# New order tables for the steady passes of a two-block transformer kernel

## The chip, the cores and the metric

One core of one Trainium2 chip runs the kernel. The time is device microseconds (us) of one execution. Three runs of the kernel before gave a median of 767.87 us (767.48 to 768.92). The trace is of one profiled execution of 767.54 us.

## The reference

Two transformer blocks work on 8 batches of 256 tokens with 256 channels. Each block adds attention and a feed-forward layer, both of the same normalised input, to its residual.

```python
xn = _layernorm(x, axis=-1)
x = x + _L0_attn_ref(xn, ...) + _L0_ffn_ref(xn, ...)
xn = _layernorm(x, axis=-1)
x = x + _L1_attn_ref(xn, ...) + _L1_ffn_ref(xn, ...)
```

- Block 0 attention: 16 heads of 16 channels, scores with an ALiBi bias and a causal mask, softmax clamped at 1e-10, output projection.
- Block 0 feed-forward: 8 experts, `silu(x @ Wg) * (x @ Wu) @ Wd`, summed with router weights that come from a sigmoid, two exponentials and a top-2 choice.
- Block 1 attention: 16 heads, causal, with biases.
- Block 1 feed-forward: two ternarised linear layers (256 to 1024 to 256) with an exact GELU between them. Its output is quantised with the largest magnitude over all batches, so that part comes at the very end.

## The kernel before, in words

The work of one batch is cut into named **steps**, and each engine (PE = TensorE matmuls, DVE = VectorE, ACT = ScalarE, POOL = GpSimd, SP = SyncE, which issues the DMAs) does its own part of each step. A step's parts are tied by semaphores only, so the order in which an engine takes its steps is free as long as nothing waits in a circle. This order is written out by hand: `ORDER_TEXT` has for each of tensor, vector, scalar and gpsimd four lists, `first`, `steady`, `last` and `final`. `run_passes` runs `first` once, `steady` six times in a loop, then `last` and `final`. SP follows the tensor list.

A steady pass is software-pipelined: it holds block 0 of batch n, block 1 of batch n-1, and, marked with `+`, the start of block 0 of batch n+1. Every engine takes its list strictly in order, and the loop goes round from the list's end to its head.

The number behind a step's name in the text does not bind: `in_turn` sorts the steps of one name and writes them back into that name's places. `score:5 norm:1 score:6` at a list's head therefore means score 0, norm 0, score 1. Only the sequence of names counts.

The steps that matter here:

- `ln1a`, `ln1b`: layer norm statistics (DVE), the power for 1/std and the bias sum (POOL), the normalising (DVE, line 1370). `ln1a` needs the last `down` of the pass before. `tr1` turns the result on PE (line 1085); ACT copies it to `xt_hi` (954), DVE takes the remainder `xt_lo` (1375). `q1`, `k1` (1111), `w1` (1160) and `v1` (1124) read both.
- `score`: PE computes two heads at a time (1193, 1195), the pair counted on the even step; DVE adds the bias and takes row maxima (1524), ACT exponentiates (1013). A pair's matmuls wait until DVE has read the pair before. `norm` (DVE, 1546 and 1549), `turn` (PE transposes, 1203 to 1205, and an ACT copy, 1022), `value` (PE, 1253) follow. `b` is block 1's first score round (DVE line 1538), `s` its second (PE 1222 to 1228, ACT 1041, a POOL mask 865), `m` and `mp` carry its row maxima, `y` its values (PE 1253 and 1259, DVE reciprocal 1557).
- `gate`, `up` (PE 1138; ACT tanh 990; DVE 1470 and 1475; ACT 994; POOL 856) and `down` (PE 1149; DVE 1486): one expert each, 0 to 7. `rt1` (DVE 1403 to 1410) and `rt2` (two ACT exponentials, 985 and 986, then 21 small DVE instructions, 1425 to 1464): the router.
- `q0`, `k0`: matmuls, then ACT (971, 974); `l0` and `l1`: DVE splits queries and keys into two halves (1380), SP stores them to DRAM (672, 675) and loads them back in another layout, four DMAs for heads 0 to 7 and four for heads 8 to 15 (690). `score` 0 waits for the first four of `l0`, `b` 0 for those of `l1`.
- `op0`, `op1`: output projections (PE 1180). `op1` ends the pass on PE and waits for the DVE part of `y:3`.
- `xe`: POOL copies the transposed input for the experts (851, 852); `gate` 0 waits for it.

Steps in `BANKED` share three PSUM buffers `gen_ps` in turn, in the order of the tensor list: a step's matmuls wait until the step three places earlier in that sequence has been read.

Of the kernel before, what the change touches and what calls it, by code (L numbers as in the profile page):

```python
# [74 lines left out]
def in_turn(items, key):  # L75
# [3 lines left out]
    for item in items:  # L79
# [8 lines left out]
            ln0a ln0b setup split xe split:1 setup:2 vsplit tr0 split:2 split:3 l0 q0 v0 split:5 k0 gate setup:1 rt1  # L88
            v0:1 norm:1 up gate:1 score norm split:4 rt2 score:1 up:1 split:6 down score:2 turn:1 gate:2 score:3
            split:7 norm:2 down:1 score:4 turn up:2 gate:3 score:5 norm:3 norm:4 split:9 up:3 gate:4 turn:2 split:8  # L90
            score:6 tern down:2 norm:6 norm:5 turn:3 tmx split:10 value score:8 tern:1 turn:4 down:3 norm:7 turn:5
            norm:8 split:11 score:7 up:4 tern:6 turn:6 score:10 score:9 norm:9 turn:7 score:11 score:12 turn:9
            norm:11 gate:5 tern:2 down:4 norm:10 turn:8 value:1 norm:12 score:13 split:13 turn:10 tern:3 split:12
            +ln0a tern:4 up:5 tsm gate:6 score:14 turn:11 gate:7 +ln0b up:6 down:5 norm:14 score:15 turn:12 norm:15
            turn:13 tern:5 value:2 tmx:1 norm:13 up:7 tern:8 +tr0 vsplit:1 down:6 turn:14 tern:7 +q0 +k0 +v0 tern:9
            +l0 turn:15 value:3 +xe +v0:1 op0 down:7 tsm:1 tern:10 tern:11
        """,
        "steady": """
            gate ln1a score score:1 score:2 norm:1 norm:2 ln1b norm up tr1 turn score:3 turn:1 score:4 norm:3 q1 rt2
            score:5 k1 norm:4 score:6 turn:2 gate:1 down h1 up:1 turn:3 gate:2 w1 norm:5 rt1 w1:2 w1:3 l1 w1:1 v1  # L100
# [9 lines left out]
            score:4 down score:5 norm:4 turn:2 turn:1 up:1 score:6 turn:3 gate:2 score:7 v1 w1 w1:1 w1:2 norm:5 w1:3  # L110
            up:2 l1 norm:6 turn:4 h1 score:8 value down:1 turn:5 norm:7 gate:3 norm:8 turn:6 score:9 norm:9 score:10
            turn:7 down:2 score:11 turn:8 norm:10 value:1 score:12 norm:11 turn:9 h1:1 h1:2 score:13 norm:12 gate:4
            b turn:10 up:3 turn:11 score:14 turn:12 score:15 norm:13 value:2 norm:14 b:1 norm:15 turn:13 up:4 b:2
            turn:14 gate:5 h1:3 turn:15 b:3 mp down:3 value:3 b:4 up:5 m down:4 gate:6 b:5 up:6 gate:7 up:7 s b:6
# [25 lines left out]
            gate rt2 score:1 tr1 score:2 gate:1 score turn up score:3 q1 k1 score:5 turn:1 score:4 turn:2 up:1  # L140
            score:6 gate:2 w1:2 w1 turn:3 w1:1 w1:3 score:7 turn:4 up:2 score:8 turn:5 gate:3 h1 turn:7 turn:6
            score:11 score:10 score:9 value:1 turn:8 score:12 h1:1 turn:11 score:14 h1:2 turn:9 turn:10 score:13
            up:3 gate:4 score:15 turn:15 turn:13 turn:12 gate:5 turn:14 h1:3 up:5 value:3 up:4 m gate:6 gate:7 s
            up:6 up:7 s:1 s:2 m:1 s:3 +tr1 s:5 s:4 +q1 +k1 s:6 s:7 +w1 +w1:2 +w1:3 +w1:1
        """,
        "final": """
            h1:2 h1:1 h1 h1:3 m quant:1 quant s s:1 s:2 quant:4 m:1 quant:2 s:6 quant:3 s:4 s:5 quant:6 quant:7 s:7
            quant:5 s:3
# [4 lines left out]
            ln0a split setup ln0b split:1 vsplit tr0 setup:2 split:2 v0 l0 gate rt1 v0:1 up split:4 gate:1 score  # L153
            score:1 up:1 norm rt2 norm:2 split:6 score:2 down gate:2 score:3 norm:1 score:4 down:1 norm:3 up:2
            split:8 gate:3 score:5 norm:4 up:3 tern score:6 norm:5 tmx tern:1 gate:4 score:7 down:2 split:10 score:8
            norm:6 norm:7 down:3 score:9 up:4 norm:8 score:11 score:10 norm:9 score:12 norm:11 tern:2 gate:5 down:4
            score:13 +ln0a up:5 norm:10 norm:12 split:12 tsm tern:5 tern:6 score:14 gate:6 norm:13 up:6 +ln0b
# [6 lines left out]
            score:10 gate:3 score:11 norm:9 down:1 norm:10 b up:3 score:12 norm:11 score:13 down:2 norm:12 score:14
            score:15 norm:13 down:3 norm:14 b:1 norm:15 b:2 gate:4 up:4 b:3 +ln0a b:4 w2 +ln0b gate:5 b:5 down:4 op0
            b:6 +tr0 up:5 b:7 gate:6 +l0 up:6 y:1 gate:7 up:7 down:5 +v0 down:6 y:3 +v0:1 down:7 op1
        """,
        "last": """
            score:1 ln1a score gate rt1 ln1b rt2 score:2 norm tr1 up score:3 gate:1 norm:1 score:4 norm:2 score:5
            norm:3 down up:1 score:6 norm:5 gate:2 v1 l1 norm:4 score:7 up:2 norm:6 score:8 score:9 norm:7 down:1  # L170
            norm:8 score:11 gate:3 score:10 down:2 norm:10 norm:9 score:13 score:12 norm:11 norm:12 b up:3 score:14
            score:15 norm:14 norm:13 b:1 gate:4 norm:15 b:3 up:4 b:2 gate:5 down:3 b:4 up:5 down:4 b:5 gate:6 up:6
            gate:7 up:7 b:6 down:5 op0 down:6 b:7 down:7 +ln1a +ln1b w2 +tr1 y:1 +l1 y:3 op1
# [1466 lines left out]
```

## Time and profile before

| | |
|---|---|
| median of 3 runs | 767.87 us (767.48 to 768.92) |
| profiled execution, its span | 767.54 us, 765.6 us |
| PE busy | 650.1 us (85%) |
| DVE busy | 564.8 us (74%) |
| ACT busy | 465.8 us (61%) |
| POOL busy | 268.8 us (35%) |
| DMA | 56.72 MB, mean 74 GB/s |
| chain that ended last | PE 57%, DVE 14%, ACT 13%, issue 8%, DMA 3% |
| mean granted TensorE clock | 0.948 of full |

The span runs from the first instruction to the last; the execution's own time has 1.9 us around it. The chain that ended last is the one sequence of work and waits that sets the end; shares in it add up to the span, while busy shares of the engines overlap. PE's busy time counts the modelled tail of each matmul, so it is an upper bound on its work. The granted clock is the share of full speed that the chip allowed TensorE.

### The profile page before, as it was taken

How to read it: one execution, taken by the hardware profiler on the slowest of the kernel's cores; microseconds unless marked ns; L12 is line 12 of the kernel's file. 1: busy time of each engine (PE TensorE's matmuls, PEld its weight loads, DVE VectorE, ACT ScalarE, POOL GpSimd, SP SyncE). 2: the span in 40 equal slices, each digit the busy share in tenths (PEclk: the TensorE clock that was granted, in tenths of full speed). 3: DMA queues.
4: the chain of work that ended last, by engine and by line, in shares of the span. 5: the costliest groups of instructions: out<-in, count | busy, mean ns of one | idle time of the engine just before them, and what ended most of it. 6: DMA issues, size and time to landing. Idle time of an engine off the chain costs nothing.

```text
span 765.6 us, 19944 instructions
## 1 busy us (share of the span) xinstructions
PE 650.1 (85%) x6455; PEld 482.5 (63%) x6455; DVE 564.8 (74%) x2201; ACT 465.8 (61%) x1223; POOL 268.8 (35%) x386
## 2 busy tenths in 40 slices
PE   1476777989889997999899997999799988999854
PEld 1354565767666775777676776677577766767522
DVE  4479777886688859796779758795879668886364
ACT  2558756955379355965398436946487436954533
POOL 7836541223404241243313331324213341134335
PEclk9979797999999999999999999999999998999969
DMA  7743012301303030301211030302121030300552
GB/s 210 262 127 118 7 62 64 107 6 36 111 5 110 14 110 27 110 0 68 82 55 55 14 110 27 110 14 92 45 78 31 24 114 1 111 3 15 172 173 83
DMA packets 49539, 56.72 MB, mean 74 GB/s; under 512 B 5088, under 2 KB 40032, under 8 KB 49504
## 3 DMA queue, kind: packets, MB, share of 16 engines
q1 hardware_dynamic: 46464, 52.44, 21.4%
q0 software_dynamic: 1056, 2.62, 1.1%
q10 hardware_dynamic: 1984, 1.21, 0.6%
q8 instruction: 19, 0.31, 0.2%
q14 instruction: 16, 0.13, 0.1%
HBM read 33.71 MB, written 22.54 MB: 73 GB/s over the span
## 4 chain that ended last, share of the span: by engine, by line
PE 57%; DVE 14%; ACT 13%; issue 8%; DMA 3%; ACTq 1%; SPq 1%; POOL 1%; DVEq 1%; POOLq 0%
PE gen_ps L1138 16%; PE gen_ps L1149 9%; PE gen_ps L1111 6%; PE value_ps L1253 5%; PE gen_ps L1180 3%; PE gen_ps L1169 3%; ACT probs L1013 3%; ACT hid L1001 3%; PE value_ps L1259 2%; DVE probs L1524 2%; PE score_ps L1193 2%; DVE probs L1549 2%; DMA gu_lo<-x_dram 2%; PE turn_ps L1222 2%; PE turn_ps L1203 1%
## 5 line engine op out<-in xcount | busy, mean ns | idle before, releaser
L856 POOL TENSOR_TENSOR h_lo<-hid,h_hi 128x512 f16<-128x512 f32 x64 | 74.5, 1164 | 280.4 <-ACT h_hi L994 280.4
L1013 ACT ACTIVATE probs<-probs,nmax 128x256 f32<-128x256 f32 (+1 forms) x256 | 113.5, 447 | 25.6 <-DVE nmax L1524 25.1
L1138 PE MATMUL gen_ps<-xe_hi,gu_hi 128*128 128x256 f16 x512 | 101.8, 282 | 2.2 <-issue 2.2
L1138 PE MATMUL gen_ps<-xe_lo,gu_hi 128*128 128x256 f16 x512 | 101.6, 282 | 0.0
L1138 PE MATMUL gen_ps<-xe_hi,gu_lo 128*128 128x256 f16 x512 | 101.5, 281 | 0.0
L1524 DVE CUSTOM_DVE_ANT_0 probs<-score_ps,bias 128x256 f32<-128x256 f32 (+1 forms) x256 | 79.4, 352 | 16.1 <-PE score_ps L1195 15.4
L1538 DVE CUSTOM_DVE_ANT_0 junk<-score_ps,bias 128x256 bf16<-128x256 f32 (+1 forms) x256 | 76.0, 354 | 20.5 <-PE score_ps L1195 17.8
L1041 ACT ACTIVATE et<-turn_ps 128x384 f32<-128x384 f32 x128 | 55.7, 489 | 46.9 <-PE turn_ps L1228 42.9
L990 ACT ACTIVATE tanh_sb<-gen_ps 128x512 f32<-128x512 f32 x64 | 37.9, 591 | 70.9 <-PE gen_ps L1138 70.9
L1549 DVE TENSOR_SCALAR probs<-probs,rsum 128x256 f32<-128x256 f32 (+1 forms) x256 | 76.4, 341 | 4.5
L865 POOL TENSOR_SCALAR_AFFINE_SELECT et<-et 128x256 f32<-128x256 f32 x128 | 50.8, 419 | 67.5 <-ACT et L1041 67.4
L1193 PE MATMUL score_ps<-k_stack,q_stack 64*128 64x256 f16 x256 | 37.0, 285 | 41.5 <-DVE nmax L1524 20.2
L1022 ACT ACTIVATE pt<-turn_ps 128x384 f32<-128x384 f32 x128 | 60.4, 482 | 18.9 <-PE turn_ps L1205 18.7
L1149 PE MATMUL gen_ps<-wd_hi,h_hi 128*128 128x256 f16 x256 | 50.8, 281 | 9.4 <-issue 6.8
L1193 PEld LDWEIGHTS score_ps<-k_stack,q_stack 64*128 64x128 f16 x256 | 12.4, 93 | 71.3 <-DVE nmax L1524 24.7
L1138 PEld LDWEIGHTS gen_ps<-xe_hi,gu_hi 128*128 128x128 f16 x512 | 48.0, 101 | 14.4 <-issue 8.3
L1486 DVE SCALAR_TENSOR_TENSOR acc<-gen_ps,w,acc 128x256 f32<-128x256 f32 x112 | 48.8, 478 | 11.1 <-PE gen_ps L1149 11.0
L1138 PEld LDWEIGHTS gen_ps<-xe_hi,gu_lo 128*128 128x128 f16 x512 | 51.7, 101 | 7.4
L1138 PEld LDWEIGHTS gen_ps<-xe_lo,gu_hi 128*128 128x128 f16 x512 | 51.7, 101 | 7.4
L1475 DVE SCALAR_TENSOR_TENSOR hid<-gated,gen_ps 128x512 f32<-128x512 f32 x64 | 43.8, 685 | 12.0 <-PE gen_ps L1138 10.9
L1470 DVE SCALAR_TENSOR_TENSOR gated<-tanh_sb,gen_ps 128x512 f32<-128x512 f32 x64 | 43.7, 683 | 10.3 <-ACT tanh_sb L990 10.2
L1149 PE MATMUL gen_ps<-wd_hi,h_lo 128*128 128x256 f16 x256 | 50.6, 281 | 0.0
(210 smaller groups left out, 1640.3 us busy)
## 6 DMA issues: line engine op xcount, KB each, us to landing
scr_q<-parts SPq DMA_DIRECT2D x32, 256.0 KB, 2.8
scr_k<-parts SPq DMA_DIRECT2D x32, 256.0 KB, 3.0
q_stack<-scr_q SPq DMA_DIRECT2D x64, 128.0 KB, 3.0
k_stack<-scr_k SPq DMA_DIRECT2D x64, 128.0 KB, 3.1
x<-in_x SPq DMA_DIRECT2D x8, 256.0 KB, 2.7
y_dram<-yx_sb SPq DMA_DIRECT2D x7, 256.0 KB, 2.1
x_dram<-yx_sb SPq DMA_DIRECT2D x7, 256.0 KB, 2.2
out_dram<-gu_hi SPq DMA_DIRECT2D x7, 256.0 KB, 2.2
```

The source lines that it names most:

```text
L856: pool.tensor_tensor(h0_lo[:, e], hid0[:, e], h0_hi[:, e], ALU.subtract).then_inc(s_h0l, 1)
L865: pool.affine_select(out=on_diagonal, in_=on_diagonal, compare_op=ALU.is_ge, fill=0.0, base=0, pattern=[[0, NT], [1, P]], channel_multipli ...
L1013: last = act.activation(probs[:, k, lo:hi], probs[:, k, lo:hi], ACT.Exp, scale=-1.0, bias=nmax[:, k, j:j + 1], accum_out=esum[:, k, j:j + 1])
L1022: act.activation(pt[:, slot:slot + 3].rearrange("p t q -> p (t q)"), turn_ps[s % 2][:, 0:3 * P], ACT.Copy).then_inc(s_ev[0], 1)
L1041: act.activation(et[:, s % TURNED], turn_ps[hp][:, 0:3 * P], ACT.Exp).then_inc(s_ev[1], 1)
L1138: last = pe.matmul(g[:, S * f:S * f + S], w[:, st.arg, m, k, cols], xx[:, k, :], start=(i == 0), stop=(i == len(terms) - 1))
L1149: last = pe.matmul(g[:, D * t:D * t + D], h[:, st.arg % 2, f, P * t:P * t + P], w[:, st.arg, f, :], start=(i == 0), stop=(i == len(terms) ...
L1193: pe.matmul(score_ps[hp][:, 0:S], q[rows[hp], i, P:S], k[rows[hp], i, :], start=True, stop=True)
L1486: dve.scalar_tensor_tensor(acc[:, t], g[:, D * t:D * t + D], w8[:, t, e:e + 1], (xb[0] if st.place == 0 else acc)[:, t], ALU.mult, ALU.add)\
L1524: last = dve.tensor_tensor_reduce(out=probs[:, k, lo:hi], in0=g[:, lo:hi], in1=bias0[:, s, blo:S], scale=-1.0, scalar=BIG, op0=ALU.add, op ...
L1538: last = dve.tensor_tensor_reduce(out=junk[:, hp, lo:hi], in0=score_ps[hp][:, lo:hi], in1=bias1[:, blo:S], scale=-1.0, scalar=BIG, op0=ALU ...
L1549: last = dve.tensor_scalar(probs[:, k, lo:hi], probs[:, k, lo:hi], rsum[:, k, j:j + 1], CLAMP, ALU.mult, ALU.max)
```

## The change

Only the four `steady` lists change in content; the words of `first`, `last` and `final` are the same and only wrapped at another column. No instruction is added or taken away, and no wait is rewritten: each step keeps its own waits and comes at another place in its engine's list. The lines of the changed kernel are numbered 7 higher from the end of the tables on. A line or two of each list, which tell how such lists read:

```diff
     "tensor": {
         "steady": """
-            gate ln1a score score:1 score:2 norm:1 norm:2 ln1b norm up tr1 turn score:3 turn:1 score:4 norm:3 q1 rt2
-            score:5 k1 norm:4 score:6 turn:2 gate:1 down h1 up:1 turn:3 gate:2 w1 norm:5 rt1 w1:2 w1:3 l1 w1:1 v1
...
+            score:5 norm:1 score:6 gate score:2 tr1 score:3 up q1 turn:1 score ln1b norm:7 turn k1 norm:2
+            norm score:11 gate:1 norm:5 rt2 score:1 down up:1 ln1a l1 gate:2 norm:3 turn:2 h1 w1 w1:2
...
     "scalar": {
         "steady": """
-            gate score score:1 score:2 tr1 up turn rt2 turn:1 score:3 q1 k1 score:4 turn:2 gate:1 score:5 score:6
...
+            gate score rt2 tr1 score:1 score:5 score:6 up score:3 q1 gate:1 k1 turn:3 score:4 turn score:2
...
     "vector": {
         "steady": """
-            ln1a score:1 score gate ln1b norm:1 score:2 norm rt1 up score:3 tr1 score:6 norm:2 score:4 rt2 norm:3
...
+            ln1a score:2 score:1 ln1b rt1 score:3 gate tr1 norm:1 norm:2 score:4 up score score:6 rt2
...
     "gpsimd": {
         "steady": """
-            ln1a up up:1 h1 up:2 h1:2 h1:1 h1:3 up:3 up:4 mp +ln0a s:3 s mp:1 up:5 s:4 s:2 up:6 s:1 s:7 s:5 +xe s:6
-            up:7
+            ln1a up:4 up:2 h1:1 up h1:3 up:1 h1 h1:2 mp +ln0a s:5 up:3 s:6 s:4 up:5 mp:1 s:2 s:1 up:6 s:7
+            s:3 s up:7 +xe
```

With the numbers put in turn, the heads of the lists read as follows. Tensor before: gate, score 0 and 1, score 2 and 3, up, tr1, turn 0, turn 1, score 4 and 5, q1, k1. Tensor after: score 0 and 1, gate, score 2 and 3, tr1, up, q1, turn 0, score 4 and 5, turn 1, k1, gate 1, score 6 and 7, down 0, up 1, gate 2, turn 2, w1 0, w1 1, turn 3, w1 2, turn 4, w1 3. Vector after, from the list's head: ln1a, score 0, score 1, ln1b, rt1, score 2, gate, tr1, norm 0, norm 1, score 3, up, score 4, score 5, rt2, score 6, gate 1, norm 2, down 0, up 1, l1, norm 3, gate 2. The tensor list's end (from up 7 on) before: up 7, s 6, y 2, s 7, v0, down 6, y 3, down 7, v0 1, op1; after: up 7, y 2, s 7, down 6, v0, y 3, down 7, v0 1, op1.

Three places, as the built programs have them (REGISTER_ALU and ISA rows without names set up a wait or count; names with a number are buffers):

PE at the loop's head, before: the end of `gate` (line 1138), then the first pair of heads (1193, 1195).

```order
L1138 MATMUL gen_ps0<-xe_hi,gu_hi 128x256 x2
L1138 MATMUL gen_ps0<-xe_lo,gu_hi 128x256 x2
L1138 MATMUL gen_ps0<-xe_hi,gu_lo 128x256 x2
L337 ISA x2
L1193 MATMUL score_ps0<-k_stack00,q_stack00 128x256
L1193 MATMUL score_ps1<-k_stack00,q_stack00 128x256
L1195 MATMUL score_ps0<-k_stack00,q_stack00 128x128
L1195 MATMUL score_ps1<-k_stack00,q_stack00 128x128
```

PE at the loop's head, after: the same pair first, then `gate`.

```order
L1200 MATMUL score_ps0<-k_stack00,q_stack00 128x256
L1200 MATMUL score_ps1<-k_stack00,q_stack00 128x256
L1202 MATMUL score_ps0<-k_stack00,q_stack00 128x128
L1202 MATMUL score_ps1<-k_stack00,q_stack00 128x128
L344 ISA x2
L1145 MATMUL gen_ps0<-xe_hi,gu_hi 128x256 x2
L1145 MATMUL gen_ps0<-xe_lo,gu_hi 128x256 x2
L1145 MATMUL gen_ps0<-xe_hi,gu_lo 128x256 x2
```

The pair, which waits for the loaded stacks, has moved from behind `gate` to the first place of the pass.

DVE in front of `tr1`, before: `up` (hid0), score 3, then the remainder `xt_lo`.

```order
L1475 SCALAR_TENSOR_TENSOR hid0<-gated,gen_ps1 128x512
L337 REGISTER_ALU
L1524 ISA probs,nmax<-score_ps1,bias0 128x256
L1524 ISA nmax 128x1
L1524 ISA probs,nmax<-score_ps1,bias0 128x128
L1375 TENSOR_TENSOR xt_lo<-gen_ps2,xt_hi 128x512
```

DVE in front of `tr1`, after: score 2, `gate` (gated), then `xt_lo`.

```order
L1531 ISA probs,nmax<-score_ps0,bias0 128x256
L1531 ISA nmax 128x1
L1531 ISA probs,nmax<-score_ps0,bias0 128x128
L344 ISA
L344 REGISTER_ALU
L1477 SCALAR_TENSOR_TENSOR gated<-tanh_sb,gen_ps0 128x512
L1382 TENSOR_TENSOR xt_lo<-gen_ps1,xt_hi 128x512
```

`up`, score 3 and the two norms no longer stand between `ln1b` and `xt_lo`; `rt1`, score 2 and `gate` do.

ACT late in the pass, before: one `s` step (et), then `q0` and `k0` back to back (rest, parts).

```order
L1041 ACTIVATE et<-turn_ps0 128x384
L1041 ACTIVATE et<-turn_ps1 128x384
L337 REGISTER_ALU
L971 ACTIVATE rest<-gen_ps0,bqk0 128x256 x2
L337 REGISTER_ALU
L974 ACTIVATE parts<-rest 128x512
L971 ACTIVATE rest<-gen_ps1,bqk0 128x256 x2
```

ACT late in the pass, after: the end of `s` 5, `k0`, then `s` 6.

```order
L1048 ACTIVATE et<-turn_ps0 128x384
L1048 ACTIVATE et<-turn_ps1 128x384
L978 ACTIVATE rest<-gen_ps1,bqk0 128x256 x2
L344 REGISTER_ALU
L981 ACTIVATE parts<-rest 128x512
```

`k0` has moved from behind `q0` and ahead of `s` 3 to behind `s` 5, so `l0` and its eight loads come later.

## Rows read from the trace of the kernel before

**Rows 1.** Windows, one steady pass: stretch, length, busy us (instructions) per engine, PEclk, DMA.

```profile
253.66:338.36 84.70, 78.69 (x808) 59.14 (x808) 65.13 (x269) 53.80 (x149) 25.61 (x40) 0.98 0.18 59
```

**Rows 2.** Waits of PE in that pass: waiter <- releaser: us, times, longest.

```profile
PE score_ps L1193 <- DVE nmax L1524: 3.2, 2, 1.9
PE turn_ps L1203 <- DVE probs L1549: 0.6, 1, 0.6
PE score_ps L1193 <- DVE nmax L1538: 0.5, 1, 0.5
PE gen_ps L1160 <- ACT hid L1001: 0.5, 1, 0.5
PE value_ps L1253 <- ACT pt L1022: 0.4, 1, 0.4
PE gen_ps L1111 <- DVE xt_lo L1375: 0.3, 1, 0.3
PE gen_ps L1180 <- DVE at L1559: 0.3, 1, 0.3
```

**Rows 3.** Timeline of PE, head of a pass: start, us, work [idle before <- releaser].

```profile
289.04 1.99 PE L1180 MATMUL gen_ps<-wo_sb,at 128*128 128x256 f32 x8 [0.32 <-DVE at L1559]
...
294.48 0.28 PE L1193 MATMUL score_ps<-k_stack,q_stack 64*128 64x256 f16 x2 [1.88 <-DVE nmax L1524]
...
294.75 0.39 PE L1138 MATMUL gen_ps<-xe_hi,gu_hi 128*128 128x256 f16 x2
...
296.07 0.60 PE L1085 MATMUL gen_ps<-ident,acc 128*128 128x128 f32 x4
296.51 0.27 PE L1203 MATMUL turn_ps<-ident,probs 128*128 128x128 f32 x1
...
300.19 0.39 PE L1111 MATMUL gen_ps<-xt_hi,qk_hi 128*128 128x256 f16 x2 [0.34 <-DVE xt_lo L1375]
```

**Rows 4.** Timeline of DVE, the same head of the pass.

```profile
294.35 0.68 DVE L1470 SCALAR_TENSOR_TENSOR gated<-tanh_sb,gen_ps 128x512 f32<-128x512 f32 x1
294.95 0.72 DVE L1370 TENSOR_SCALAR acc<-acc,mv,rstd 128x256 f32<-128x256 f32 x2
295.60 0.15 DVE L1546 RECIPROCAL rsum<-esum 128x2 f32<-128x2 f32 x1
...
296.25 0.42 DVE L1524 CUSTOM_DVE_ANT_0 probs<-score_ps,bias 128x256 f32<-128x256 f32 x1
...
297.46 0.17 DVE L1403 TENSOR_SCALAR r_in<-r_tanh 128x16 f32<-128x16 f32 x1
...
298.22 0.69 DVE L1475 SCALAR_TENSOR_TENSOR hid<-gated,gen_ps 128x512 f32<-128x512 f32 x1
...
299.37 0.69 DVE L1375 TENSOR_TENSOR xt_lo<-gen_ps,xt_hi 128x512 f16<-128x512 f32 x1
```

**Rows 5.** Timeline of DVE, the router `rt2`, the step behind it, and a `down`.

```profile
301.82 0.29 DVE L1425 TENSOR_TENSOR r_gt<-r_e 128x128 f32<-128x128 f32 x1
...
305.46 0.16 DVE L1546 RECIPROCAL rsum<-esum 128x2 f32<-128x2 f32 x1
...
309.11 0.87 DVE L1486 SCALAR_TENSOR_TENSOR acc<-gen_ps,w,xb 128x256 f32<-128x256 f32 x2
```

**Rows 6.** Windows, one microsecond of `q1` and `k1` (columns as above).

```profile
301.00:302.00 1.00, 1.00 (x7) 0.69 (x6) 1.00 (x7) 0.48 (x4) 0.00 (x0) 0.50 0.00 0
```

**Rows 7.** The chain that ended last: start, us, work; `q1` with `k1`, two passes.

```profile
300.19 4.46 PE gen_ps L1111 x24
...
384.89 2.79 PE gen_ps L1111 x24
```

**Rows 8.** Timeline of DVE and SP: `l0` and its fourth stack load.

```profile
357.34 1.23 DVE L1380 TENSOR_TENSOR parts<-rest,parts 128x1024 f16<-128x1024 f32 x1 [2.68 <-ACT parts L974]
...
364.96 0.60 SPq L690 DMA_DIRECT2D k_stack<-scr_k  x1
```

**Rows 9.** The page's DMA issues: KB each, median us from issue to landing.

```profile
k_stack<-scr_k SPq DMA_DIRECT2D x64, 128.0 KB, 3.1
```

More of the change, by code:

```diff
@@ L87 @@
         "first": """
[L88 to L96, printed above, removed]
+            ln0a ln0b setup split xe split:1 setup:2 vsplit tr0 split:2 split:3 l0 q0 v0 split:5 k0 gate
@@ L107 @@
+            score:14 turn:7 down:2 turn:11 value:1 turn:10 score:13 turn:8 down:3 norm:14 mp:1 b:1 turn:13
+            gate:4 turn:12 b:2 value:2 h1:3 up:4 turn:14 norm:4 b:3 turn:15 w2 b:4 m gate:5 value:3 s +ln0a
+            b:5 op0 s:1 b:6 up:5 +tr0 norm:10 score:15 gate:6 s:2 h1:1 b:7 down:4 up:6 +q0 gate:7 m:1 +ln0b
+            s:3 y +k0 s:4 y:1 s:5 mp down:5 s:6 up:7 y:2 +l0 s:7 down:6 +v0 y:3 down:7 +v0:1 op1 +xe
         """,
         "last": """
-            ln1b ln1a rt1 score:2 gate score rt2 tr1 norm norm:2 norm:1 up gate:1 score:3 turn q1 k1 score:1 norm:3
@@ L110 @@
[L110 to L114, printed above, removed]
@@ L115 @@
-            down:5 op0 s:1 mp:1 b:7 down:6 down:7 s:2 +ln1a y s:3 +ln1b m:1 w2 +tr1 s:4 y:1 s:6 +q1 +k1 +l1 s:5 y:2
-            s:7 +w1 y:3 +w1:3 +w1:2 +w1:1 op1
+            ln1b ln1a rt1 score:2 gate score rt2 tr1 norm norm:2 norm:1 up gate:1 score:3 turn q1 k1 score:1
+            norm:3 score:4 down score:5 norm:4 turn:2 turn:1 up:1 score:6 turn:3 gate:2 score:7 v1 w1 w1:1
+            w1:2 norm:5 w1:3 up:2 l1 norm:6 turn:4 h1 score:8 value down:1 turn:5 norm:7 gate:3 norm:8
+            turn:6 score:9 norm:9 score:10 turn:7 down:2 score:11 turn:8 norm:10 value:1 score:12 norm:11
@@ L117 @@
+            turn:9 h1:1 h1:2 score:13 norm:12 gate:4 b turn:10 up:3 turn:11 score:14 turn:12 score:15
+            norm:13 value:2 norm:14 b:1 norm:15 turn:13 up:4 b:2 turn:14 gate:5 h1:3 turn:15 b:3 mp down:3
+            value:3 b:4 up:5 m down:4 gate:6 b:5 up:6 gate:7 up:7 s b:6 down:5 op0 s:1 mp:1 b:7 down:6
+            down:7 s:2 +ln1a y s:3 +ln1b m:1 w2 +tr1 s:4 y:1 s:6 +q1 +k1 +l1 s:5 y:2 s:7 +w1 y:3 +w1:3 +w1:2
+            +w1:1 op1
         """,
         "final": """
-            h1:2 h1:3 v1 fetch h1 mp b b:1 w2 quant:5 b:2 b:4 ymx mp:1 h1:1 qmax b:5 m quant b:3 b:7 s fetch:1 b:6
@@ L138 @@
         """,
         "last": """
[L140 to L144, printed above, removed]
+            gate rt2 score:1 tr1 score:2 gate:1 score turn up score:3 q1 k1 score:5 turn:1 score:4 turn:2
@@ L152 @@
         "first": """
[L153 to L157, printed above, removed]
@@ L164 @@
[L164 to L166 removed]
+            ln1a score:2 score:1 ln1b rt1 score:3 gate tr1 norm:1 norm:2 score:4 up score score:6 rt2
+            score:5 gate:1 norm:4 down up:1 l1 norm:8 gate:2 norm:7 score:10 norm score:9 score:11 score:8
@@ L167 @@
+            score:7 up:2 norm:3 v1 norm:6 gate:3 up:3 b norm:10 norm:9 down:1 score:12 norm:5 norm:12
+            score:14 norm:11 score:15 score:13 norm:13 b:1 down:2 norm:14 b:3 norm:15 down:3 gate:4 b:2 up:4
+            +ln0a b:4 w2 b:5 +ln0b op0 gate:5 b:6 up:5 +tr0 b:7 gate:6 down:4 up:6 gate:7 y:1 +l0 up:7
+            down:5 +v0 down:6 y:3 down:7 +v0:1 op1
         """,
         "last": """
-            score:1 ln1a score gate rt1 ln1b rt2 score:2 norm tr1 up score:3 gate:1 norm:1 score:4 norm:2 score:5
@@ L170 @@
[L170 to L173, printed above, removed]
+            score:1 ln1a score gate rt1 ln1b rt2 score:2 norm tr1 up score:3 gate:1 norm:1 score:4 norm:2
```

80 lines of the change are left out of this document (51 added, 29 removed).

## The prediction

> **What bounds the kernel now.** I read three views, in this order. First the windows of one steady pass [rows 1]: it lasts 84.70 us, and PE is busy in 78.69 of them, DVE in 65.13, ACT in 53.80, POOL in 25.61. PE is the bound, and the six steady passes, which run one list, are two thirds of the time. A reordering leaves every engine its work, so all that it can win is PE's idle time and what PE loses at a lower clock; it can lose without limit. Second, the waits of PE in that pass [rows 2]: 3.2 + 0.6 + 0.5 + 0.5 + 0.4 + 0.3 + 0.3 = 5.8 us. Third, the timelines of PE and DVE at the head of a pass [rows 3, 4], which show that most of it is one hole. `op1` ends the old pass; DVE needs its result, does `ln1a` and score 0 and 1, and only then may the second pair of heads start, 1.88 us late, at 294.48. From there DVE decides: its `xt_lo`, which `q1` waits for, starts at 299.37 only, behind `gate`, `ln1b`, two norms, score 2, `rt1`, `up` and score 3. Between 294.48 and `q1` at 300.19 PE waits 1.37 (the rest of the first line), 0.59 and 0.34 us more. The hole is 4.2 us of the 5.8.
>
> The hole has a second price. Where `q1` and `k1` follow it, the granted clock reads 0.50, the 1.2 GHz level [rows 6], after PE was idle for more than half of the stretch before, and these 24 matmuls take 4.46 us; at 2.4 GHz they take 2.79 [rows 7]. Of the six such rows of the steady passes four read 4.40 to 4.46 and two 2.79. That is 1.67 us in four passes of six, 1.1 on the mean.
>
> **Part 1, the head of the pass.** All times are laid on the pass of rows 3 and 4.
> - The second pair: DVE still does `ln1a`, score 0, score 1 first, and these depend on `op1` alone. It starts at 294.48 as before; the wait of 1.88 stays.
> - `ln1b` no longer stands behind `gate`, whose place lasted 294.95 - 294.35 = 0.60. It takes 0.65 (to 295.60) [rows 4], so it ends at 295.0. `tr1`, now directly behind the pair (which ends at 294.75 [rows 3]), starts at 295.1 and takes 0.44 (296.07 to 296.51). A wait of 0.4. Then `up`, 1.32, to 296.9.
> - DVE goes on: `rt1` 0.76 (297.46 to 298.22), a score 0.55 (`up` and score 3 take 1.15 from 298.22 to 299.37, and `up` as much as `gate`, 0.60), `gate` 0.60, so `xt_lo` starts at 296.9 and, with its 0.69, ends at 297.6 instead of 300.06. `q1` followed 0.13 behind it before, so it starts at 297.7 instead of 300.19. A wait of 0.8. ACT must have copied `xt_hi` by 296.9; its two router exponentials now stand ahead of that copy and wait for `rt1` (295.8), which leaves it 1.1 us. I cost this at nothing; if that cover goes, `xt_lo` is late by what is over.
> - `q1` takes half of 2.79, 1.4, to 299.1 [rows 7], and turn 0 about 0.3. Meanwhile DVE does two norms of 0.65 (295.60 to 296.25) and score 3: 297.6 + 1.3 + 0.55 = 299.4, so the third pair waits 0.1.
>
> The hole becomes 1.9 + 0.4 + 0.8 + 0.1 = 3.2 us instead of 4.2: **-1.0**. Bounds: -0.5, if every link adds a tenth, to -2.3, if all but the first wait goes.
>
> **Part 2, from `k1` to the second half of the pass.** Before, PE waits 0.5 + 0.5 + 0.4 = 1.4 here (all but the head's and `op1`'s in rows 2). After, turn 1 and `k1` follow the third pair, and PE is through `k1` at 301.6, some 3 us earlier than before. DVE is not so much earlier: it does score 4 and 5 by 301.2 and then `rt2`, 305.46 - 301.82 = 3.64 [rows 5], with score 6 and `gate` 1 behind it: 301.2 + 3.64 + 0.55 + 0.60 = 306.0. PE meanwhile has `gate` 1, a pair, `down` 0 and `up` 1, three of 1.32 and one of 0.3: 305.9. `gate` 2 shares a PSUM buffer with `gate` 1, so it waits 0.1 to 0.2. It and turn 2 and two `w1` (8 matmuls each, about 0.9 by the 12 of `q1`) bring PE to 309.4; turn 3 needs norm 3, before which DVE has norm 2, `down` 0 (0.87), `up` 1, `l1` (1.23 [rows 8]) and norm 3 itself: 306.0 + 0.65 + 0.87 + 0.60 + 1.23 + 0.65 = 310.0. A wait of 0.5. `gate` 2 on DVE is next and frees the buffer of the third `w1`: 0.2. After that DVE runs ahead. Together some 1.0 instead of 1.4: **-0.4**. Bounds: -1.4, if DVE gains on this, to +1.0, if each of the five steps of DVE comes 0.3 later than reckoned.
>
> **Part 3, the end of the pass.** The work from `up` 7 to `op1` is the same but for two exchanges of neighbours, and `op1` still waits for `y:3`: 0.3 as before. What moves is `l0`. Before, it ended at 357.34 + 1.23 = 358.57, and the fourth load was issued at 364.96 [rows 8] and landed about 3.1 later [rows 9], at 368.1: 9.5 us behind `l0`. This `op1` starts one pass behind that of rows 3, at 373.7, so the loads had landed 5.6 us before `op1` even began. Now `k0` comes five PE steps later (two of 1.32, three shorter) and on ACT behind `s` 4 and 5. I estimate `l0` 8 us later against `op1`: it ends 7 us ahead of it instead of 15, and the four loads land 2.5 us after `op1` starts. The first pair, now the head of the list, could go 1.9 us after (the busy time of `op1` [rows 3]). It waits 0.6, and `gate` behind it. This costs nothing: pair and `gate` take 1.7, the second pair can't go before 294.48, which is 5.4 behind `op1`, so up to 1.8 of waiting only fills the 1.88 that PE would wait anyway. Beyond 1.8, each microsecond is one of the pass.
>
> Here a rule speaks against the change. The Trainium skill, "DMA: Bandwidth & Descriptors", section "Rules for kernel authors", says to issue a DMA early, compute, and wait on its semaphore late; the new list issues later and waits earlier. The trace of a steady pass has no DMA among the waits of PE [rows 2], so it neither bears this out nor denies it. By the rule the wait counts in full, 0.6 in six passes, and the sum is 3.6 us higher; by the slack just worked out it counts zero, which I take.
>
> **Part 4, the clock.** The hole gets shorter, 3.2 us of waits between 292.6 and 297.7 in place of 4.2 between 292.6 and 300.2, yet no less idle while it lasts. No row shows whether the clock then falls. If it never does, 1.1 is won; if it falls as often and as long, nothing. If it falls within the hole, `tr1` and `up` run at the lower level, and part of that is covered by the 0.8 before `q1`. I take half: **-0.55**.
>
> **The sum.** -1.0 - 0.4 - 0.55 = -1.95 per pass, -11.7 in six. The profiled execution took 767.54 us, 0.33 below the median; 767.87 - 11.7 = 756.2, so **756 us**.
>
> **Rivals.**
> - The hole costs no clock and the middle has no waits: -1.0 - 1.4 - 1.1 = -3.5, six times -21: 747 us. For it: DVE has idle time in every pass, and a list of its own making could use it. Against: `rt2` is 3.64 in one piece just where PE runs ahead.
> - The head's gain is given back in the middle: part 2 at +1.0, part 4 at nothing: 0.0 per pass, 768 us. For it: DVE is the releaser of most waits, and its work is only put off. Against: its steps behind `rt2` are late by tenths only in the count above.
> - Slower: the first pair becomes the end of a DMA chain. `l0` stands on DVE behind `y:1`, `k0` on ACT behind two `s`, each of which waits for PE, the mask or `y`. If the stacks land 5 us later than reckoned, 0.6 + 5 - 1.8 = 3.8 is a wait at the head of PE's list with `gate` behind it: -1.95 + 3.8 = +1.85 per pass, 779 us. It decides from about 3.2 us of lateness on. For it: the spare time shrinks by the most of all in this change, and PE takes its list in order. Against: the four loads landed with a median of 3.1 us, and nothing else of size is on the queue then. It is what the rule of the Trainium skill above warns of.
> - The change does not do what it says: the numbers in the text are sorted back, so only the sequence of names moves. If what moves waits nowhere, 768 us. Against: `xt_lo` clearly moves.
>
> **How the numbers follow.** A measurement of this kernel tells differences over about 0.2%, 1.5 us, from no change. Chances: forecast 0.50 (its own range 748 to 763), the better case 0.22, given back 0.10, slower 0.14, nothing moves 0.04. Faster: 0.49 of the forecast, 0.22, and 0.03 of the given back, 0.74. Slower: 0.14, 0.03 of the given back and 0.01 of the forecast, 0.18. Same: 0.08. The range: 744, a little under the better case (the head at -1.5), to 771, part 1 at -0.5, part 2 at +1.0 and part 4 at nothing: it leaves out about two in ten, most of them the slower rival.
>
> **What would show it.** Right: in the passes of the changed kernel the second pair still waits some 1.9 us or, with the DMA wait in front of `gate`, pair and wait together the same; `xt_lo` ends 5.0 us behind the start of the second pair's wait (292.6) instead of 7.5; PE is through `k1` some 7 us behind that pair instead of 10; `q1` and `k1` together take under 4 us in more passes; pass to pass takes 82 to 83 us. Wrong: a wait of PE for `k_stack` of over 2 us per pass (the slower rival); waits of PE for norm or for `gen_ps` behind `rt2` of over 2 us per pass (given back); a pass of 81 us with the granted clock at full throughout (the better case).

## The result and the profile after

The changed kernel takes 771.16 us (median of 8 runs, 769.06 to 774.2), the kernel before 767.31 on the same chip (8 runs): a ratio of 1.0054, with an interval of 1.0028 to 1.0079. It is slower by half a per cent, and the interval does not reach 1; forecast was 756 us, faster by 1.5 per cent.

The profiled execution of the changed kernel has a span of 771.4 us, 5.8 more than before. At 774.20 us it is the longest of the eight, 3.0 above their median, so, if all of that lay in its six steady passes, they would be half a microsecond longer than usual. Its windows over a steady pass, from one `w2` (PE's matmuls of the second layer of block 1's feed-forward, once a pass) to the next (stretch, length, busy us of PE, PEld, DVE, ACT and POOL, PEclk, DMA share, GB/s), answer to [rows 1]:

```profile
422.85:508.68 85.83, 78.21 (x807) 58.09 (x807) 70.07 (x269) 54.10 (x149) 26.46 (x40) 1.00 0.18 58
```

The five intervals between the six `w2` starts of the steady passes (165.39 to 594.5) have a mean of 85.82 us, before 84.35 (168.96 to 590.7). That is 7.4 us lost; the first `w2` comes 3.6 us earlier and what follows the last takes 2.0 us more, which gives the 5.8. The lists cost 1.47 us a pass where 1.95 was to be won. PE works no longer, and its granted clock reads 1.00, the upper level, in all five passes (before 0.98 in the mean of each). What grew is DVE: 70.07 us busy against 65.13, with the same count (x269).

The waits of PE in that pass (waiter, releaser, total us, times, longest), which answer to [rows 2]:

```profile
PE turn_ps L1210 <- DVE probs L1556: 2.0, 4, 1.0
PE score_ps L1200 <- DVE nmax L1531: 2.0, 2, 1.3
PE gen_ps L1145 <- DVE gated L1477: 1.2, 1, 1.2
PE gen_ps L1118 <- DVE xt_lo L1382: 0.7, 1, 0.7
PE gen_ps L1176 <- DVE acc L1493: 0.5, 2, 0.2
PE gen_ps L1187 <- DVE at L1566: 0.4, 1, 0.4
PE score_ps L1200 <- DMA k_stack<-scr_k: 0.4, 1, 0.4
PE gen_ps L1092 <- DVE acc L1377: 0.3, 1, 0.3
PE gen_ps L1092 <- DVE gated L1477: 0.3, 1, 0.3
```

They sum to 7.8 us against 5.8. Almost all are for DVE, and the largest new ones (turns for a norm, `gate` 2 for `gated`) lie behind the head of the pass.

Which of DVE's instructions grew is seen in the groups by form (line, engine, operation, tiles, count, then busy us and mean ns). First the kernel before:

```profile
L1549 DVE TENSOR_SCALAR probs<-probs,rsum 128x128 f32<-128x128 f32 x128 | 39.5, 309 | 0.0
L1370 DVE TENSOR_SCALAR x<-x,mv,rstd 128x256 f32<-128x256 f32 x14 | 5.1, 408 | 0.0
L1425 DVE TENSOR_TENSOR r_gt<-r_e 128x128 f32<-128x128 f32 x8 | 2.3, 289 | 0.0
```

Then the changed kernel, the same groups:

```profile
L1556 DVE TENSOR_SCALAR probs<-probs,rsum 128x128 f32<-128x128 f32 x128 | 52.2, 407 | 0.0
L1377 DVE TENSOR_SCALAR x<-x,mv,rstd 128x256 f32<-128x256 f32 x14 | 10.1, 763 | 0.0
L1432 DVE TENSOR_TENSOR r_gt<-r_e 128x128 f32<-128x128 f32 x8 | 7.9, 984 | 0.0
```

The same instructions on the same tiles take longer in the mean: the 128x128 half of a `norm` (its 128x256 half grew too, from 373 to 441 ns), the scaling in `ln0b` (block 0's counterpart of `ln1b`), and the first instruction of `rt2`, more than three times as long. The timeline tells which of them, and beside what. On POOL the long instructions are the subtracts that make the low half of a hidden layer, 128x512 each: `h_lo` in the steps `up`, `h_parts` in the four steps `h1` of block 1. POOL in a steady pass of the changed kernel (start, us, work, idle time before):

```profile
385.36 1.16 POOL L863 TENSOR_TENSOR h_lo<-hid,h_hi 128x512 f16<-128x512 f32 x1 [7.05 <-ACT h_hi L1001]
...
405.55 1.16 POOL L886 TENSOR_TENSOR h_parts<-hid,h_parts 128x512 f16<-128x512 f32 x1 [3.92 <-ACT h_parts L1015]
406.67 1.15 POOL L863 TENSOR_TENSOR h_lo<-hid,h_hi 128x512 f16<-128x512 f32 x1
407.79 1.20 POOL L886 TENSOR_TENSOR h_parts<-hid,h_parts 128x512 f16<-128x512 f32 x1
411.26 1.29 POOL L863 TENSOR_TENSOR h_lo<-hid,h_hi 128x512 f16<-128x512 f32 x1 [2.27 <-ACT h_hi L1001]
```

And DVE in the same stretch:

```profile
385.45 1.22 DVE L1432 TENSOR_TENSOR r_gt<-r_e 128x128 f32<-128x128 f32 x1
...
406.24 0.42 DVE L1545 CUSTOM_DVE_ANT_0 junk<-score_ps,bias 128x256 bf16<-128x256 f32 x1
...
407.00 2.08 DVE L1556 TENSOR_SCALAR probs<-probs,rsum 128x256 f32<-128x256 f32 x2
...
409.18 0.55 DVE L1556 TENSOR_SCALAR probs<-probs,rsum 128x256 f32<-128x256 f32 x2
...
411.18 1.46 DVE L1556 TENSOR_SCALAR probs<-probs,rsum 128x256 f32<-128x256 f32 x2
```

A norm that meets nothing takes 0.55 us (409.18). The one at 407.00 begins 0.33 us into a subtract of POOL, meets the next too, and ends 0.09 us behind that (409.08 and 408.99). The one at 411.18 ends 0.09 behind POOL's 1.29 as well, `r_gt` 0.15 behind its subtract. The custom instruction at 406.24, which reads the scores from PSUM, takes its 0.42 in the middle of one. The profile shows this nowhere as a wait of DVE: the instruction is only longer. Two such instructions that run at the same time are said to meet below.

In each of the five intervals of the changed kernel four norms are so long (by 1.53, 0.91, 0.90 and 0.50 us), and `r_gt` (0.93) and `ln0b`'s scaling (1.57 instead of 0.73). In the five intervals of the kernel before not one of these is.

### The profile page after: what moved, and what is told of

Same layout as the page of the kernel before. It is cut to its first block and busy times, and to the rows that moved or that the text cites. A ratio compares the mean times of both kernels' runs of the same rounds, so it can differ in the third digit from the quotient of the medians.

```text
span 771.4 us, 19956 instructions
## 1 busy us (share of the span) xinstructions
PE 647.7 (84%) x6455; PEld 476.0 (62%) x6455; DVE 593.7 (77%) x2201; ACT 467.2 (61%) x1223; POOL 272.5 (35%) x386
## 5 line engine op out<-in xcount | busy, mean ns | idle before, releaser
L1556 DVE TENSOR_SCALAR probs<-probs,rsum 128x256 f32<-128x256 f32 (+1 forms) x256 | 97.9, 424 | 4.6
L872 POOL TENSOR_SCALAR_AFFINE_SELECT et<-et 128x256 f32<-128x256 f32 x128 | 54.5, 443 | 114.4 <-ACT et L1048 114.3
L886 POOL TENSOR_TENSOR h_parts<-hid,h_parts 128x512 f16<-128x512 f32 x32 | 37.9, 1188 | 75.1 <-ACT h_parts L1015 75.1
L1564 DVE RECIPROCAL inv<-value_ps 128x256 f32<-128x256 f32 x16 | 28.0, 1753 | 34.8 <-PE value_ps L1266 34.8
L1001 ACT ACTIVATE h_hi<-hid 128x512 f16<-128x512 f32 x64 | 40.4, 630 | 21.5 <-DVE hid L1482 18.5
```

Source lines behind the costliest of these rows:

```text
L872: pool.affine_select(out=on_diagonal, in_=on_diagonal, compare_op=ALU.is_ge, fill=0.0, base=0, pattern=[[0, NT], [1, P]], channel_multipli ...
L1556: last = dve.tensor_scalar(probs[:, k, lo:hi], probs[:, k, lo:hi], rsum[:, k, j:j + 1], CLAMP, ALU.mult, ALU.max)
```

## The experiments

The theory, A below: the new lists lay POOL's subtracts in `up` and `h1` beside those instructions of DVE that keep both ends in SBUF, and one engine has to wait for the other. (Both ends in SBUF turns out to be too wide; see the last section.) Rival B: the order itself costs it, by the waits it adds, above all `rt2` ahead of score 6 and `gate` 1. Rival C: the stack loads at the head. Each run's ratio is to the kernel before on its own chip. "A pass" is the mean of the five intervals between `w2` starts.

### POOL's subtracts made short, in both kernels

```diff
+c = 1 if st.kind == "steady" else S
-pool.tensor_tensor(h0_lo[:, e], hid0[:, e], h0_hi[:, e], ALU.subtract) ...
+pool.tensor_tensor(h0_lo[:, e, :, 0:c], hid0[:, e, :, 0:c], h0_hi[:, e, :, 0:c], ALU.subtract) ...
```

and the same in `h1`. Most of the low halves is left out by this. The changed kernel with it:

> The changed kernel, with POOL's subtracts that make h_lo and the low half of h_parts cut to one of 256 columns in the steady passes (the low halves of both hidden layers are left out there), same waits and same orders. Theory A (POOL's 1.16 us subtracts now run beside VectorE instructions that read and write SBUF, and stretch them: per pass four norms by 3.8 us together, r_gt by 0.9, ln0b by 0.8): the norms go back to 0.55 us a pair, a pass loses 3.5 to 5.5 us of its 85.8, and the time comes to 741 to 753. Rival B (the order itself costs it: rt2 ahead of score 6 and gate 1, waits that the new lists add): the norms may shorten but PE's waits move elsewhere, 766 to 771. Rival C (the stack DMA at the head of the pass): no change, 769 to 772.

And the kernel before:

> The kernel before with the same cut (one of 256 columns in the steady passes, the low halves left out there). Theory A: it has no stretched norm in its steady passes, so only its POOL waits can shorten: 760 to 768, and the changed kernel with the cut is 10 to 20 us faster than this one. Rival B: 762 to 768, and the changed kernel with the cut is no faster than this one.

Measured: the changed kernel with the cut 748.1 us (ratio 0.9747, 0.9719 to 0.9775), the kernel before with it 761.5 (0.9919, 0.9894 to 0.9944). Windows of a pass, first the changed kernel with the cut:

```profile
489.34:571.54 82.20, 78.94 (x808) 59.25 (x806) 64.75 (x269) 53.98 (x149) 14.95 (x40) 0.98 0.18 61
```

then the kernel before with the cut:

```profile
332.07:416.66 84.59, 78.58 (x810) 59.19 (x807) 65.13 (x269) 53.80 (x149) 14.32 (x40) 0.98 0.18 59
```

DVE is back at 64.75, and a subtract takes 0.20 us instead of 1.16. This splits the change in two. Without POOL's long subtracts a pass takes 82.06 us in the new order and 83.92 in the old one: **the order wins 1.86 us a pass**, where 1.95 was forecast. With the subtracts the new order's pass is 3.76 longer (85.82) and the old one's 0.43 (84.35). -1.86 + 3.76 - 0.43 is the measured +1.47, as it must be, since these are the differences of the same four passes. The medians of the runs, which are measured apart from the traces, split in the same way: -13.4, +23.1 and -5.8 us. The 0.43 is no meeting: DVE has 65.13 either way, and with the cut two passes of the five are near 83 us, before it one. Rivals B and C fall as what made it slower.

### The subtracts held back until DVE reads PSUM

Everything is computed again; the five subtracts that the expectation lists (its word is four) wait for a norm in the steady passes. The numbers are counts of norms done; `h1` waits by `H1_AFTER` in the same way.

```diff
+UP_AFTER = {2: 8, 3: 13}
+H1_AFTER = {1: 10, 2: 14, 3: 15}
+if st.kind == "steady" and st.arg in UP_AFTER:
+    wait(pool, s_nm, n.at(H, UP_AFTER[st.arg]))
...
-            ln1a up:4 up:2 h1:1 up h1:3 up:1 h1 h1:2 mp +ln0a s:5 up:3 s:6 s:4 up:5 mp:1 s:2 s:1 up:6 s:7
+            ln1a up:4 up:2 up h1:1 h1:3 up:1 h1 h1:2 mp +ln0a s:5 up:3 s:6 s:4 up:5 mp:1 s:2 s:1 up:6 s:7
```

> The changed kernel with everything computed, but four of POOL's subtracts in the middle of a steady pass wait for a norm to be done (up 2 for norm 7, h1 1 for norm 9, up 3 for norm 12, h1 2 for norm 13, h1 3 for norm 14), and up 2 stands ahead of h1 in POOL's list, so that they run beside VectorE instructions that read PSUM. Theory A: the norms go back to 0.55 us, DVE loses 3 to 3.8 us a pass, the turn waits of 12.2 us go, 752 to 762. Rival B: DVE's busy time falls but the time stays, 768 to 772; or the later h_lo holds up PE's down, over 771.

Measured: 765.0 us, ratio 0.9967 (0.9946 to 0.9988), a pass of 84.46. That is less gain than A forecast, though 1.36 us a pass. Three of the four norms are back at 0.55; the fourth takes 1.45, because `h1` 3 comes late from ACT and meets norm 15. `ln0b` is as long as before and `r_gt` in four passes of five, PE still waits 1.2 for `gated`, and a new wait of 0.7 for `h_lo` stands in front of `down`: here a wait moved POOL's work into the path of PE.

### `rt2` put back behind score 6 and `gate` 1

```diff
-            ... norm:1 norm:2 score:4 up score score:6 rt2
-            score:5 gate:1 norm:4 down ...
+            ... norm:1 norm:2 score:4 up score score:6
+            score:5 gate:1 rt2 norm:4 down ...
```

> The changed kernel with one edit in VectorE's list: rt2 stands behind score 6 and gate 1, as before the change, not ahead of them. Theory A: r_gt no longer meets POOL's subtract (0.9 us a pass back) and PE's wait of 1.2 us for gate 2 goes, the four stretched norms stay: 764 to 769. Rival B with rt2 as its cause: most of the loss comes back, 755 to 762.

Measured: 779.2 us, 1.0159 (1.0129 to 1.0189), a pass of 86.84: slower still. Both theories missed here. `r_gt` is at 0.28 again and the wait for `gate` 2 is gone, as A said, yet another wait took their place. DVE's timeline around the new place of `rt2` in this kernel:

```profile
477.85 0.42 DVE L1531 CUSTOM_DVE_ANT_0 probs<-score_ps,bias 128x256 f32<-128x256 f32 x1 [2.16 <-PE score_ps L1202]
...
478.41 0.68 DVE L1477 SCALAR_TENSOR_TENSOR gated<-tanh_sb,gen_ps 128x512 f32<-128x512 f32 x1
479.01 0.28 DVE L1432 TENSOR_TENSOR r_gt<-r_e 128x128 f32<-128x128 f32 x1
```

and PE behind it:

```profile
483.44 0.33 PE L1210 MATMUL turn_ps<-ident,probs 128*128 128x128 f32 x1 [1.68 <-DVE probs L1556]
```

DVE has nothing to do for 2.16 us, since score 6 is not there yet; in the new order `rt2` fills that gap. Behind score 6 it holds up the next norm, for which PE waits 1.68. So the new place of `rt2` is one of the things that the change gains by, worth 1.0 us a pass (86.84 against 85.82, the shorter `r_gt` counted in), and not its fault.

### The kernel before made to meet

The old order and all its work, but four of POOL's subtracts wait for the reciprocal in front of a norm (`up` 2 for the 10th, `h1` 1 to 3 for the 11th, 12th and 14th), and `up` 3 goes ahead of `h1` 3 in POOL's list.

> The kernel before with its own orders and work, but four of POOL's subtracts per steady pass are held until a reciprocal of a norm is done, so that each starts as that norm starts (up 2 with norm 9, h1 1 with norm 10, h1 2 with norm 11, h1 3 with norm 13). Theory A: each of the four norms goes from 0.55 to about 1.6 us, DVE's busy time grows by 4 us a pass, and the time by what of that is on the path, 8 to 25 us: 775 to 792. Rival B: a later h_lo costs little and a norm takes what it took, 765 to 770.

Measured: 789.8 us, 1.0283 (1.0245 to 1.0321). POOL in a pass of it:

```profile
508.68 1.15 POOL L885 TENSOR_TENSOR h_parts<-hid,h_parts 128x512 f16<-128x512 f32 x1 [1.28 <-ACT h_parts L1014]
512.68 1.16 POOL L885 TENSOR_TENSOR h_parts<-hid,h_parts 128x512 f16<-128x512 f32 x1 [2.84 <-DVE rsum L1552]
513.79 1.21 POOL L860 TENSOR_TENSOR h_lo<-hid,h_hi 128x512 f16<-128x512 f32 x1
```

and its norms:

```profile
508.64 1.54 DVE L1555 TENSOR_SCALAR probs<-probs,rsum 128x256 f32<-128x256 f32 x2
512.64 2.44 DVE L1555 TENSOR_SCALAR probs<-probs,rsum 128x256 f32<-128x256 f32 x2
```

Four norms a pass take 1.54 us or, where two subtracts follow each other, 2.44. DVE is busy 4.8 us longer a pass (69.9 against 65.1), and a pass takes 88.62, 4.3 more. The loss can be made in a kernel that did not have it. PE has no wait for `h_lo` or `h_parts` in these passes, so it is not the later subtracts that cost it. Not all of it is waiting: in the pass from 435.99 to 525.43 PE's waits sum to 8.3 us instead of 5.8, and PE is busy 81.1 us instead of 78.7, at a mean granted clock of 0.94 instead of 0.98.

### What POOL may do beside them

Copies in place of the subtracts, which read one tile and not two:

```diff
-pool.tensor_tensor(h0_lo[:, e], hid0[:, e], h0_hi[:, e], ALU.subtract) ...
+if st.kind == "steady":
+    settle(pool, s_gps)
+pool.tensor_copy(h0_lo[:, e], h0_hi[:, e]) ...
```

The same is done in `h1`; `settle` is one semaphore increment.

> The changed kernel with POOL's subtracts of h_lo and h_parts replaced by copies of the same size, fp16 to fp16, that read one tile of SBUF and not two (the low halves are wrong). Theory A, if any POOL instruction on SBUF holds up the norm: norms stretch to the end of the copy, by less only as the copy is shorter than 1.16 us; with copies of about 0.6 us 755 to 765. If it is the two reads that clash, no norm is stretched and the time is that of the cut kernel, 746 to 751. Rival B: 766 to 771.

And fills, `pool.memset(h0_lo[:, e], 0.0)` with the same `settle`, which read nothing:

> The changed kernel with POOL's subtracts of h_lo and h_parts replaced by fills with zero of the same tiles (the low halves are left out): POOL writes SBUF and reads nothing. The Trainium skill, page SBUF — State Buffer, section Who interferes with whom, says that a VectorE instruction with two SBUF inputs clashes with a GpSimd instruction that reads SBUF and not with one that only writes it, and that one in a 2-port mode clashes with any. If so, r_gt stays at 0.29 us beside a fill while norm and ln0b, which scale a tile in place, are stretched to its end. If only reads clash, nothing is stretched. The time, with fills somewhat shorter than the copies of 0.62 us: 746 to 753 in both cases.

Measured: 750.2 us with copies (0.9753, 0.9722 to 0.9785) and 749.1 with fills (0.9757, 0.9717 to 0.9797). POOL's timeline at `rt2` in the run with copies:

```profile
539.92 0.75 POOL L865 COPY h_lo<-h_hi 128x512 f16<-128x512 f16 x1 [7.14 <-ACT h_hi L1004]
```

DVE's, same run and place:

```profile
539.91 0.29 DVE L1435 TENSOR_TENSOR r_gt<-r_e 128x128 f32<-128x128 f32 x1
540.12 0.70 DVE L1437 TENSOR_TENSOR r_eq<-r_e 128x128 f32<-128x128 f32 x1
```

POOL's timeline in the run with fills, at `rt2` and at a norm:

```profile
292.90 0.53 POOL L865 MEMSET h_lo<- 128x512 f16 x1 [7.13 <-ACT h_hi L1004]
...
316.95 0.53 POOL L865 MEMSET h_lo<- 128x512 f16 x1 [3.33 <-ACT h_hi L1004]
```

DVE's, same run:

```profile
292.91 0.29 DVE L1435 TENSOR_TENSOR r_gt<-r_e 128x128 f32<-128x128 f32 x1
293.11 0.29 DVE L1437 TENSOR_TENSOR r_eq<-r_e 128x128 f32<-128x128 f32 x1
...
316.86 0.95 DVE L1559 TENSOR_SCALAR probs<-probs,rsum 128x256 f32<-128x256 f32 x2
```

A copy that starts 0.01 us behind `r_gt` leaves it alone and stretches the next instruction, `r_eq`, from 0.29 to 0.70, to 0.15 behind the copy's end (so in three passes of five; in the other two neither meets a copy). A fill beside both leaves both at 0.29, but stretches a norm to 0.95. So the comparisons of `rt2`, which read both operands from SBUF, clash with the two POOL instructions that read and not with the one that only writes; the scaling in place clashes with all three. Norms are long beside copies too (0.71, 0.91 and 0.91 a pass), so it does not take two reads on POOL. The time with copies was below A's range: POOL's instruction is shorter (0.62 us in the mean instead of 1.18), three norms a pass are long instead of four, and DVE is busy 66.0 us a pass instead of 70.1.

### Towards a better list

The run with held-back subtracts, with its remaining meetings taken apart by order. Its added waits stay; parts of the lists, against those of the changed kernel:

```diff
 scalar
-... score:5 score:6 up score:3 ...
+... score:5 up score:6 score:3 ...
-... h1 turn:14 score:12 score:14 turn:10 gate:4 h1:1 ...
+... h1 h1:1 turn:14 score:12 score:14 turn:10 gate:4 ...
 vector
-... score:4 up score ...
+... up score:4 score ...
 gpsimd
-ln1a up:4 up:2 h1:1 up h1:3 up:1 h1 h1:2 mp +ln0a s:5 up:3 s:6 s:4 ...
+ln1a up:4 up:2 up h1:1 up:1 h1:3 h1 h1:2 mp +ln0a s:5 s:6 up:3 s:4 ...
 tensor
-... turn:8 down:3 norm:14 mp:1 b:1 ...
+... turn:8 b:1 down:3 norm:14 mp:1 ...
```

> The third run's kernel with its remaining meetings taken apart by order alone: up ahead of score 3 in VectorE's and ScalarE's lists (so that h_lo 0 is through before rt2 begins), h1 3 right behind h1 2 in ScalarE's list, up 4 behind the second s in POOL's, b 1 ahead of down 3 in TensorE's. Everything is computed. Theory A: DVE has no stretched norm and no stretched r_gt in a steady pass, the pass comes from 84.46 near the 82.2 of the cut kernel, 82.3 to 83.5, and the time to 750 to 760. Rival B (the order itself costs it): no better than 764.

Measured: 757.0 us, 0.985 (0.9826 to 0.9874), a pass of 83.10. `r_gt` and `ln0b` are back at their old length. One norm a pass was still 1.11 long, since `h1` 1 had slipped behind `up` 3 in POOL's list. Put back (`up:2 up h1:1 h1:3 up:1`):

> The fifth run's kernel with h1 1 back ahead of up 3 in POOL's list, which takes away its last stretched norm (1.11 us, once a pass, h1 1 beside norm 13). Theory A: the norms are at 0.55 us throughout the steady passes, a pass loses 0 to 0.6 of its 83.1 us, 753 to 758. Rival: that norm lay beside other waits of PE and b 1's new place costs as much, 757.

Measured: 758.6, 0.9877 (0.9839 to 0.9914), a pass of 83.11: no norm is long any more, and nothing is won by it, as the rival said. Then with TensorE's list left as in the changed kernel:

> The run before this one with TensorE's list as the changed kernel has it (down 3 ahead of b 1). In the fifth run PE waited 0.96 us a pass for nmax ahead of b 1; in the third it waited 0.73 for h_lo ahead of down 3. Theory A does not tell these apart: within 3 us of the run before, and nearer 753 if the wait for nmax was the dearer.

Measured: 753.9, 0.9837 (0.9796 to 0.9877), a pass of 83.01. The intervals of the last two overlap and the passes differ by 0.1, so TensorE's edit is undecided. This is the fastest complete kernel of the study, 1.6% below the kernel before. A pass of it:

```profile
330.10:413.08 82.98, 77.70 (x808) 58.20 (x806) 64.76 (x269) 53.88 (x149) 26.26 (x40) 1.00 0.19 60
```

DVE is at 64.76, the figure of the cut kernel, with all of POOL's work done: no norm, `r_gt` or `ln0b` is long in any of its five passes. Last, the list edits of this run without any of the added waits:

> The changed kernel with the list edits of the run before on ScalarE, VectorE and POOL and none of the added waits: what the tables alone can mend. Theory A: r_gt and ln0b go back (1.8 us a pass of DVE), some of the four norms still meet a subtract, since nothing holds POOL back: 757 to 768. Rival B (the order costs it): 768 to 772.

Measured: 761.6, 0.9933 (0.991 to 0.9957), a pass of 83.81. The tables alone mend `r_gt`, `ln0b` and one norm of four; three still take 1.31 to 1.46.

## Why the prediction was wrong

By its steps:

- **"A reordering leaves every engine its work"** is the step that failed, and with it every duration of DVE in part 2. It holds for what is issued and not for how long an instruction takes: DVE's work in a pass grew from 65.1 to 70.1 us. The sum has no term for POOL: the prediction gives its 25.61 us of work and says nothing of its list, which the change rewrites too, nor of what DVE does beside it.
- **Part 2**, the middle, forecast at 1.0 us of waits, has 4.7: the 7.8 above less 2.7 at the head and 0.4 at `op1`. `rt2`, taken as 3.64 from [rows 5], lasted 4.72 (385.45 to the score at 390.17), and `gate` 2 waited 1.2 for what was to be 0.1 to 0.2. The prediction's own sign for "given back" (over 2 us a pass of waits for a norm or for `gen_ps` behind `rt2`) came true, 2.0 and 1.2. It was nearest by its time too, 768, but by luck: its mechanism, work that is only put off, is not what happened, for with the subtracts cut the waits of a pass sum to 3.1 to 3.8.
- **Part 1**, the head, was right: forecast 3.2, measured 0.4 for the stack, 1.3 for the second pair, 0.3 for `tr1`, 0.7 for `q1` and nothing for the third pair, 2.7.
- **Part 3** was right: PE waits 0.4 for the stack (forecast 0.6), and over the five passes this wait (0 to 0.4) and the one behind it (1.3 to 1.6) sum to 1.6 to 1.7, in place of the second pair's old 1.88, so it costs nothing. The slower rival did not occur; the result is slower, as it said, for another reason. The Trainium skill, "DMA: Bandwidth & Descriptors", section "Rules for kernel authors", says to issue a DMA early and to wait for it late. The 0.6 a pass that the prediction priced by it was not felt at this size.
- **Part 4** was right in kind and half as large as it came: the clock stays at 1.00 in all five passes of the changed kernel, which by the prediction's own price wins the whole 1.1 and not half of it (PE's busy time, which counts overlapping tails, falls by 0.40). With the subtracts cut it still falls in four passes of five, now inside the hole: two matmuls of `up` take 0.63 there instead of 0.38 (285.80 and 450.14 in that run); such a pass is 0.72 longer (82.20 against 81.48). In the old order with the cut three passes of five are 1.68 longer (84.59 against 82.91).
- **The sum**, -1.95 a pass, is near what the order gives with the subtracts cut, -1.86, and in its parts too: 1.43 between the short passes of the two cut kernels (82.91 and 81.48) where 1.4 of waits was forecast, the other 0.43 from falls of the clock where 0.55 was. The missing term is the 3.76 that POOL's long subtracts cost in the new order. Of this 2.81 comes back when all of them are done and none meets (83.01, in a kernel that also moves a few steps of ACT and DVE). Of the 0.95 left, 0.7 may be the wait for `h_lo` that PE has there and not in the cut kernel; no run shows it. The range ended at 771 and the result lies just past it; no rival held a longer instruction.

The Trainium skill has the rule, on "SBUF — State Buffer", section "Who interferes with whom": VectorE and GpSimd share one pair of SBUF ports. A VectorE instruction in a 2-port mode contends for it (`tensor_scalar` is named among those that can enter one), and one with two SBUF inputs contends with a GpSimd instruction that reads SBUF, not with one that only writes it. Whoever issues first holds the pair for the whole instruction. The rows above agree, for subtracts, copies and fills; which mode a norm runs in, no row shows.

The prediction did not draw on it, though the trace of the kernel before has the sign of it in five of its six steady passes, in the very hole that the prediction took apart. There `ln1a` adds a constant to a 128x2 tile in SBUF. The instruction takes 0.17 us where POOL is idle or ends its work as it starts (630.46), and 0.41 or 0.42 where it starts inside POOL's addition `xb`. It then ends 0.02 to 0.04 behind that:

```profile
292.91 0.41 DVE L1360 TENSOR_SCALAR var<-mv 128x2 f32<-128x2 f32 x1
...
630.46 0.17 DVE L1360 TENSOR_SCALAR var<-mv 128x2 f32<-128x2 f32 x1
```

POOL beside the first, and its subtract that starts 0.31 behind a norm, which takes 1.25 where the others take 1.16:

```profile
291.90 1.40 POOL L820 TENSOR_TENSOR xb<-acc,ob_sb 128x256 f32<-128x256 f32 x2 [6.14 <-DVE yx_sb L1512]
...
320.54 1.25 POOL L879 TENSOR_TENSOR h_parts<-hid,h_parts 128x512 f16<-128x512 f32 x1 [2.94 <-ACT h_parts L1008]
```

The change adds meetings of the same kind, with longer instructions.

## What to carry to other kernels

When a change moves work on GpSimd or VectorE, list which of their instructions will run at the same time, and not only who waits for whom: here a meeting with one subtract costs VectorE up to 1.0 us, with two in a row up to 1.9, and no wait shows it. Look for it as the same instruction at two lengths in a timeline, in the trace of before as well, or a mean that grew in the groups by form. The repair is to place GpSimd's SBUF work beside VectorE instructions that read PSUM, by the lists first and by a wait where the lists don't hold it.
